# A LoRA block on one core: weights that arrive transposed, activations turned in transpose mode, a split shared with GpSimd

## The chip, the cores and the metric

One core of a Trainium2 chip runs the kernel. The metric is the device time of one execution in microseconds; the time before is the median of 3 runs. TensorE is PE in the profile, with PEld for its weight loads; VectorE is DVE, ScalarE is ACT, GpSimd is POOL, and SyncE, which issues most transfers, is SP.

## What is computed

Eight sequences of 128 tokens with 512 features (`x`) pass through four adapter layers. Each sequence picks its own adapter. All data is float32.

```python
w = L0_weight[id0]                          # (8, 512, 512), one matrix per sequence, stored (out, in)
x = x + einsum('bsi,boi->bso', x, w)        # layer 0; the result is x1 below
# layer 1: q, k, v = x1 @ W + (x1 @ A[id1]) @ B[id1];  q, k turned by rope(pos);  causal, masked softmax; out projection
x = x + attention(x, mask, pos, id1)
x = x + einsum('bnr,bor->bno', einsum('bni,bri->bnr', x, L2_B[id0]), L2_A[id0])     # layer 2, rank 16
x = x + x @ L3_W.T + L3_b + 2 * (x @ L3_As[id2]) @ L3_Bs[id2]                       # layer 3, rank 16
```

## The kernel before

Every large product is made of three fp32r products of TensorE, each of a high and a low half: `hi*hi + hi*lo + lo*hi`. The high half is a copy to fp32r by ScalarE, the low half is the difference, by VectorE or GpSimd. So every operand passes through a "split". TensorE contracts over partitions, so a matrix whose rows are the wrong way round is first "turned": four matmuls of a 128x128 tile against an identity into one PSUM bank, from which the split reads.

The program has four blocks, one after the other, each closed by a barrier over the engines. Every engine has its own instruction order, written out by hand, and engines wait for each other by semaphores.

**Stage one (layer 0 and the preparation of layer 1).** The loop runs over b, the eight sequences, in a software pipeline. On PE, step b is: turn x and the weight of sequence b+1 (`transposes`, line 277, into the ring `ps_ring` of three banks: five "tiles", x and the four column blocks of the weight), `product(b)` (lines 288 to 290, twelve matmuls of 512 columns), turn x1 of b-1 (line 298), `adapters(b-2)` (lines 309 to 311) and `turn_ax(b-3)` (line 321). ScalarE makes all five high halves of a sequence (line 347), VectorE all five low halves (line 401); they read the PSUM ring. Between these VectorE makes rope tables: `angles` reduces the angle in seven passes over 128x1024 for the sine, and once more in eight passes, with a quarter turn added, for the cosine. SP loads the weights (1 MB each) into two buffers `w0_raw`; the load for b waits until the weight of b-2 has been turned. It also loads x, three adapter pieces of 32 KB per sequence in rows of 64 bytes (`a_raw`), and after b = 4 the first block of layer 1's weights and adapters (`raw_w`, `raw_b`, 1 MB each). GpSimd only issues transfers here: 16 gathers of `bk` and `bv` rows, then 16 gathers of `bq` and `ao` (256 KB each) from DRAM to DRAM, as fast as it can.

**Stage two** projects k and v, **stage three** (lines 787 to 1135) is the attention loop over 8 heads by 8 sequences. Neither is touched by the change, but for a table read.

**The last stage** does layers 2 and 3. On PE: gather of the adapter rows (1264), turns of layer 3's weight and of `l2b_sel` (1238), a small product m of the adapters (1272), the product c (1280 to 1284) into one bank, eight products of the out adapter (1289), eight turns of x2 (1238), then `narrow` (1257 to 1303) and the eight wide products (1308 to 1315). VectorE has in order: the low halves of `w3t`, `bo_pack` (1384), the copy `cm` of c (1407), the eight sums into `res` (1363), the low halves of x2 (1412), `m_pack` (1415), `own` (1371). GpSimd makes `l3a_lo` (1436) and adds the bias (1441).

Of the kernel before, what the change touches and what calls it, by code (L numbers as in the profile page):

```python
# [31 lines left out]
def program(nc, x, lora_ids, pos, attn_ids, slot_ids, mask, w0, wq, wk, wv, wo, aq, bq, ak, bk, av, bv, ao, bo,  # L32
            l2a, l2b, w3, b3, l3a, l3b, ident_c, causal_c, rope_c, gather_c, twin_c, out):
# [13 lines left out]
    R = aq.shape[2]  # L47
# [20 lines left out]
    with whole:  # L68
# [34 lines left out]
        l2b_sel = sb(whole, "l2b_sel", [P, HID])  # L103
        l2a_sel = sb(whole, "l2a_sel", [P, KC, B, R])
        l3a_sel = sb(whole, "l3a_sel", [P, KC, B, R])
# [15 lines left out]
        rope_cols = sb(attn, "rope_cols", [P, 3])  # L121
# [34 lines left out]
        with ExitStack() as c:  # L156
# [14 lines left out]
            ps_ring = [ps(c, f"ps_ring{i}", [P, HID]) for i in range(3)]  # L171
            ps_y = [ps(c, f"ps_y{i}", [P, HID]) for i in range(2)]
            ps_x1 = ps(c, "ps_x1", [P, KC, T])
# [15 lines left out]
            tile_ready = sem(c, "tile_ready")  # L189
            tile_hi_done = sem(c, "tile_hi_done")  # L190
            tile_lo_done = sem(c, "tile_lo_done")
# [14 lines left out]
            TILES = 1 + KC  # L206

            with nc.Block() as block:
                @block.sync
                def _(sp):  # L210
# [3 lines left out]
                    for b in range(B):  # L214
                        a = sp.value_load(id_rows[0:1, 0, b:b + 1], min_val=0, max_val=w0.shape[0] - 1)
                        if b >= 2:

                            sp.wait_ge(tile_ready, TILES * (b - 1))
                        src = w0[bass.DynSlice(a, 1), :, :].rearrange("a (c p) i -> p (a c) i", p=P)
                        if b == 0:  # L220

                            for k in range(KC):
                                cols = slice(k * P, (k + 1) * P)
                                sp.dma_start(w0_raw[0][:, :, cols], src[:, :, cols]).then_inc(w0_first_in[k], 16)
# [5 lines left out]
                        pick = sp.value_load(id_rows[0:1, 1, b:b + 1], min_val=0, max_val=aq.shape[0] - 1)  # L230
                        for n, src in enumerate((aq, ak, av)):
                            sp.dma_start(a_raw[:, b, :, n, :],
                                         src[bass.DynSlice(pick, 1)].rearrange("a (c p) r -> p (a c) r", p=P)).then_inc(a_in[b], 16)
# [8 lines left out]
                def _(pool):  # L242
# [1240 lines left out]
```

## Time and profile before

| | before |
|---|---|
| median of 3 runs | 849.56 us (848.63 to 849.73) |
| span of the profiled execution | 850.1 us |
| TensorE busy | 797.7 us, 94% |
| VectorE, ScalarE, GpSimd busy | 621.6, 363.9, 307.9 us |
| stage one | 0 to 106 us |
| stages two and three | 106 to 782 us |
| last stage | 782 to 850 us |

The profiled execution has no time of its own beside its span; the span, 850.1 us, is 0.5 us above the median of the runs. A row of instruction groups reads: line, engine, operation, output <- input, shapes, count | busy us, mean ns of one | idle us just before them and what ended it. A float32 matmul stands as two records, an fp32r one as one. A row of busy time by stretch reads: the stretch, its length, busy us (instructions) of PE, PEld, DVE, ACT and POOL, the granted TensorE clock as a share of full speed, the busy share of the 16 DMA engines, GB/s. A row of a timeline: start us, us from the first to the last instruction merged in it, engine, line, operation, names, shapes, count, and in brackets the idle time before it and what ended it.

### The profile page before, as it was taken

The page shows a single profiled execution, that of the slowest core. Times are in us where ns is not written, and L with a number is a line of the kernel's source. Part 1 is how long each engine was busy: PE and PEld are TensorE (multiplying, and loading weights), DVE is VectorE, ACT ScalarE, POOL GpSimd, SP SyncE. Part 2 cuts the span into 40 slices and gives each one's busy share as a digit, 9 for nine tenths or more (in the row PEclk, how much of TensorE's full clock was granted, in tenths as well). Part 3 has the DMA queues.
Part 4 walks back from the last instruction along what each step waited for, and adds up shares of the span by engine and source line. Part 5 has one row for each costly group of instructions (what it writes and reads, how often), then busy time and mean ns, then how long its engine had stood idle before and what let it go on. Part 6 is the DMA issues. An engine that isn't in the chain of part 4 may idle for free. (4 is left out here: it accounts for less than half of the span.)

```text
span 850.1 us, 14916 instructions
## 1 busy us (share of the span) xinstructions
PE 797.7 (94%) x4780; PEld 674.6 (79%) x4780; DVE 621.6 (73%) x1556; ACT 363.9 (43%) x989; POOL 307.9 (36%) x261
## 2 busy tenths in 40 slices
PE   5699898999779999999999999999999999987898
PEld 5599786778568888888888888888888888865786
DVE  2568652488669789779779878878877977864783
ACT  3245442311054446446446446446445544543450
POOL 5300030044455336337336426435524632510220
PEclk9899999999989999999999999999999999999899
DMA  9992178887405123313304402602512211601302
GB/s 270 315 276 57 46 195 225 225 218 205 136 2 130 44 63 72 104 42 81 111 0 118 116 0 67 168 0 62 135 38 62 62 37 43 128 7 35 94 13 86
DMA packets 112750, 86.89 MB, mean 102 GB/s; under 512 B 60534, under 2 KB 79126, under 8 KB 112454
## 3 DMA queue, kind: packets, MB, share of 16 engines
q1 hardware_dynamic: 110770, 79.83, 35.7%
q0 software_dynamic: 1792, 6.49, 2.3%
q8 instruction: 21, 0.34, 0.2%
q14 instruction: 19, 0.16, 0.1%
q10 hardware_dynamic: 148, 0.07, 0.0%
HBM read 71.40 MB, written 20.73 MB: 108 GB/s over the span
## 5 line engine op out<-in xcount | busy, mean ns | idle before, releaser
L935 POOL TENSOR_TENSOR prob<-prob,rinv 128x512 f32<-128x512 f32 x64 | 66.7, 1042 | 198.6 <-DVE rinv L1025 198.6
L880 ACT ACTIVATE prob<-sm,nmax 128x128 f32<-128x128 f32 x256 | 99.8, 391 | 81.0 <-DVE nmax L1006 81.0
L928 POOL TENSOR_TENSOR qt<-qc,qs 128x512 f32<-128x512 f32 x60 | 96.0, 1599 | 94.8 <-DVE qs L964 94.8
L1102 PE MATMUL ps_out<-wo_hi,ot_hi 128*128 128x512 f32 x256 | 106.2, 415 | 5.4 <-DVE ot_lo L983 3.7
L1104 PE MATMUL ps_out<-wo_hi,ot_lo 128*128 128x512 f32 x256 | 100.6, 393 | 0.0
L82 PE MATMUL ps_q<-x1t_hi,blk_hi 128*128 128x512 f32 x240 | 100.5, 419 | 0.0
L1103 PE MATMUL ps_out<-wo_lo,ot_hi 128*128 128x512 f32 x256 | 99.6, 389 | 0.0
L1006 DVE CUSTOM_DVE_ANT_0 sm<-ps_s,maskbias 128x128 f32<-128x128 f32 x256 | 58.7, 284 | 53.8 <-issue 53.8
L83 PE MATMUL ps_q<-x1t_lo,blk_hi 128*128 128x512 f32 x240 | 95.5, 398 | 0.0
L84 PE MATMUL ps_q<-x1t_hi,blk_lo 128*128 128x512 f32 x240 | 95.2, 397 | 0.0
L964 DVE TENSOR_TENSOR qs<-ps_q,sin_t 64x512 f32<-64x512 f32 x120 | 82.6, 688 | 3.7
L869 ACT ACTIVATE ot_hi<-ps_o 128x512 fp32r<-128x512 f32 x64 | 38.1, 595 | 105.5 <-PE ps_o L1090 105.3
L1070 PEld LDWEIGHTS ps_s<-kt,qt 128*128 128x128 f32 x512 | 68.5, 195 | 11.0 <-issue 5.4
L1070 PE MATMUL ps_s<-kt,qt 128*128 128x128 f32 x512 | 69.2, 279 | 5.2 <-PEq L563 5.2
L1035 DVE TENSOR_TENSOR p_lo<-prob,p_hi 128x512 f16<-128x512 f32 x64 | 60.9, 951 | 5.9 <-ACT p_hi L896 4.1
L1102 PEld LDWEIGHTS ps_out<-wo_hi,ot_hi 128*128 128x128 f32 x256 | 48.1, 188 | 14.4 <-DVE ot_lo L983 4.9
L1104 PEld LDWEIGHTS ps_out<-wo_hi,ot_lo 128*128 128x128 f32 x256 | 48.0, 188 | 11.3
L863 ACT ACTIVATE pt_hi<-ps_t 128x512 fp32r<-128x512 f32 x64 | 38.3, 599 | 42.7 <-PE ps_t L1080 42.7
L1103 PEld LDWEIGHTS ps_out<-wo_lo,ot_hi 128*128 128x128 f32 x256 | 48.4, 189 | 8.5
L84 PEld LDWEIGHTS ps_q<-x1t_hi,blk_lo 128*128 128x128 f32 x240 | 45.4, 189 | 10.9
L896 ACT ACTIVATE p_hi<-prob 128x512 f16<-128x512 f32 x64 | 40.1, 627 | 29.0 <-POOL prob L935 28.8
L82 PEld LDWEIGHTS ps_q<-x1t_hi,blk_hi 128*128 128x128 f32 x240 | 45.7, 191 | 8.4
(207 smaller groups left out, 1937.1 us busy)
## 6 DMA issues: line engine op xcount, KB each, us to landing
wo_raw<-in_L_cond_wo SPq DMA_DIRECT2D x8, 1024.0 KB, 5.6
raw_w<-in_L_cond_wq SPq DMA_DIRECT2D x8, 1024.0 KB, 6.8
w_raw<-in_L_cond_weight SPq DMA_DIRECT2D x7, 1024.0 KB, 6.6
raw_b<-bq_sel SPq DMA_DIRECT2D x56, 128.0 KB, 4.6
raw_b<-bkv_sel SPq DMA_DIRECT2D x16, 256.0 KB, 6.7
v_hi_d<-v_hi SPq DMA_DIRECT2D x16, 256.0 KB, 3.7
v_lo_d<-v_lo SPq DMA_DIRECT2D x16, 256.0 KB, 4.9
k_rot<-kr SPq DMA_DIRECT2D x16, 256.0 KB, 2.6
```

Source lines behind the costliest of these rows:

```text
L82: pe.matmul(bank[:, :], w_hi[:, k, cols], x1t_hi[:, k, tok], start=(k == 0), stop=False)
L83: pe.matmul(bank[:, :], w_hi[:, k, cols], x1t_lo[:, k, tok], start=False, stop=False)
L84: pe.matmul(bank[:, :], w_lo[:, k, cols], x1t_hi[:, k, tok], start=False, stop=False)
L880: e = act.activation(prob[i][:, h, :], sm[:, h, :], ACT.Exp, bias=nmax[i][:, h:h + 1], scale=-1.0, accum_out=rsum[i][:, h:h + 1])
L928: pool.tensor_tensor(qt[:, half, h, :], qc[:, :], qs[:, :], ALU.add).then_inc(q_done, 1)
L935: pool.tensor_tensor(prob[i][:, :, :], prob[i][:, :, :], rinv[i][:, :].unsqueeze(2).broadcast_to([P, G, T]), ALU.mult).then_inc(prob_done, 1)
L964: dve.tensor_tensor(qs[to:to + 64, :], ps_q[i][at:at + 64, :], sin_t[to:to + 64, tok], ALU.mult).then_inc(q_mult, 1)
L1035: dve.tensor_tensor(p_lo[:, :, :], prob[i][:, :, :], p_hi[:, :, :], ALU.subtract).then_inc(p_lo_done, 1)
L1070: mm = pe.matmul(ps_s[b % 2][:, h, :], qt[:, half, h, at:at + T], kt[:, b * T:(b + 1) * T], start=True, stop=True)
L1102: pe.matmul(ps_out[:, :], ot_hi[:, q], wo_hi[:, h, :], start=(h == 0), stop=False)
L1103: pe.matmul(ps_out[:, :], ot_hi[:, q], wo_lo[:, h, :], start=False, stop=False)
L1104: pe.matmul(ps_out[:, :], ot_lo[:, q], wo_hi[:, h, :], start=False, stop=(h == G - 1))
```

## The change

- The host lays four tensors out as the core wants them: layer 0's weights (`w0t`), layer 3's weight (`w3t`) and layer 2's B transposed, and all adapter pieces in chunks, so that a partition's data is one run (8 KB for a weight; 768 bytes for the three adapter pieces, now one transfer). The turns of these weights on PE are gone, and their splits read SBUF, not PSUM.
- The turns of x, x1 and x2 stay, now as `pe.transpose` and not as a matmul with the identity. x and x1 have two PSUM banks each.
- Low halves of layer 0's weight: VectorE makes blocks 0 and 2, GpSimd blocks 1 and 3. The load of weight b waits for both low halves of b-2. GpSimd's gathers now stand between these, two sequences' worth behind each pair of low halves: `bk`, `bv` in steps 0 to 3, `bq`, `ao` in steps 4 to 7.
- The first block of layer 1 is loaded after b = 5 and not 4.
- The cosine is made from the sine's angle, sin(pi/2 - |angle|): one more pass on VectorE in place of eight.
- Last stage: no turns of `w3` and `l2b`; GpSimd makes `l2b_lo`.

```diff
                     for b in range(B):
-                            sp.wait_ge(tile_ready, TILES * (b - 1))
-                        src = w0[bass.DynSlice(a, 1), :, :].rearrange("a (c p) i -> p (a c) i", p=P)
+                            sp.wait_ge(wt_lo_done, 2 * (b - 1))
+                            sp.wait_ge(wt_lo_pool, 2 * (b - 1))
+                        src = w0t[bass.DynSlice(a, 1), :, :, :].rearrange("a p c o -> p (a c) o")
...
-                        if b == 4:
+                        if b == 5:
                             sp.wait_ge(gathered_kv, 2 * B * 16)
                             load_block_w(sp, 0)
                             load_block_b(sp, 0)
...
                     for b in range(B):
-                        a = pool.value_load(id_rows[0:1, 1, b:b + 1], min_val=0, max_val=bq.shape[0] - 1)
-                        pick = bass.DynSlice(a, 1)
-                        pool.dma_start(bkv_sel[b:b + 1, :, 0, :], bk[pick]).then_inc(gathered_kv, 16)
-                        pool.dma_start(bkv_sel[b:b + 1, :, 1, :], bv[pick]).then_inc(gathered_kv, 16)
...
+                        for k in (1, 3):
+                            pool.wait_ge(wt_hi_done, KC * b + k + 1)
+                            pool.tensor_tensor(wt_lo[b % 2][:, k, :], w0_raw[b % 2][:, k, :], wt_hi[b % 2][:, k, :].bitcast(F32),
+                                               ALU.subtract).then_inc(wt_lo_pool, 1)
+                        for n in (2 * b, 2 * b + 1):
+                            if n < B:
+                                gather_kv(n)
+                            else:
+                                gather_qo(n - B)
...
-                                mm = pe.matmul(ps_ring[m % 3][:, n * P:(n + 1) * P], src, ident[:, :], start=True, stop=True)
...
+                            mm = pe.transpose(ps_x[b % 2][:, k * T:(k + 1) * T], res[:, b, k * P:(k + 1) * P], ident[:, :])
...
                         for k in range(KC):
-                            pe.wait_ge(tile_lo_done, TILES * b + k + 2)
+                            if k % 2 == 0:
+                                pe.wait_ge(wt_lo_done, 2 * b + k // 2 + 1)
+                            else:
+                                pe.wait_ge(wt_lo_pool, 2 * b + k // 2 + 1)
...
                     pe.wait_ge(w3_in, 48)
...
-                    for k in range(KC):
-                        turn(k, [raw_w[:, o, k * P:(k + 1) * P] for o in range(KC)])
                     pe.wait_ge(l2_in, 32 * B)
-                    turn(L2B, [l2b_sel[:, k * P:(k + 1) * P] for k in range(KC)])
```

PE's order at the start of stage one, in the kernel before (`w_raw` is `w0_raw`; the second x and its weight are turned ahead of the first product):

```order
L277 MATMUL ps_ring<-ident,res 128x128 x4
L277 MATMUL ps_ring<-ident,w_raw 128x128 x16
L277 MATMUL ps_ring<-ident,res 128x128 x4
L277 MATMUL ps_ring<-ident,w_raw 128x128 x16
L288 MATMUL ps_y<-wt_hi,xt_hi 128x512
L289 MATMUL ps_y<-wt_lo,xt_hi 128x512
L290 MATMUL ps_y<-wt_hi,xt_lo 128x512
```

The same place in the changed kernel, with the waits:

```order
L281 MATMUL ps_x<-ident,res 128x128 [waits x_in1]
L281 MATMUL ps_x<-ident,res 128x128 x3
L295 MATMUL ps_y<-wt_hi,xt_hi 128x512 [waits wt_lo_done,xt_lo_done]
L296 MATMUL ps_y<-wt_lo,xt_hi 128x512
L297 MATMUL ps_y<-wt_hi,xt_lo 128x512
L295 MATMUL ps_y<-wt_hi,xt_hi 128x512 [waits wt_lo_pool]
L296 MATMUL ps_y<-wt_lo,xt_hi 128x512
```

Sixteen matmuls of weight turns per sequence are gone from PE, and every second group of three in a product waits for GpSimd. GpSimd's own order in the changed kernel, one step with a `bk`, `bv` pair of gathers (`TENSOR_LOAD` reads the adapter's number, `DMA` issues a gather):

```order
L262 TENSOR_TENSOR wt_lo<-w_raw,wt_hi 128x512 [waits wt_hi_done] x2
L243 TENSOR_LOAD id_rows
L243 ISA x2
L245 ISA
L245 DMA bkv_sel<-in_L_cond_bk 16x1024
L246 DMA bkv_sel<-in_L_cond_bv 16x1024
L243 TENSOR_LOAD id_rows
L243 ISA x2
L245 ISA
L245 DMA bkv_sel<-in_L_cond_bk 16x1024
L246 DMA bkv_sel<-in_L_cond_bv 16x1024
L262 TENSOR_TENSOR wt_lo<-w_raw,wt_hi 128x512 [waits wt_hi_done] x2
```

Before, this stretch held the gathers alone. Now two subtractions stand ahead of each two sequences' gathers, and the next subtractions behind them. PE in the last stage, in the changed kernel; before, 20 turns stood ahead of these rows:

```order
L1287 MATMUL ps_h<-w3t_hi,l2a_hi 128x512 [waits w3t_lo_done]
L1288 MATMUL ps_h<-w3t_lo,l2a_hi 128x512
L1289 MATMUL ps_h<-w3t_hi,l2a_lo 128x512
L1291 MATMUL ps_h<-ident,l2a_sel 128x128 x4
L1296 MATMUL ps_wide<-bo_pack,axo_pack 128x512 [waits bo_lo_done] x3
L1296 MATMUL ps_wide<-bo_pack,axo_pack 128x512 [waits wide_done,bo_lo_done] x5
```

The product c now follows the splits, which wait only for the data in SBUF.

## Rows read from the trace of the kernel before

**Rows 1.** Busy time by stretch: stage one and the last stage

```profile
0.00:106.00 106.00, 85.50 (x600) 79.92 (x600) 62.96 (x119) 42.09 (x90) 18.86 (x40) 0.95 0.66 192
782.00:850.00 68.00, 61.73 (x356) 52.13 (x356) 42.97 (x74) 22.88 (x46) 11.27 (x9) 0.95 0.25 71
```

**Rows 2.** Groups by form, PE, stage one: the weight turns

```profile
L277 PE MATMUL ps_ring<-ident,w_raw 128*128 128x128 f32 x256 | 34.1, 296 | 13.5 <-DMA w_raw<-in_L_cond_weight 12.9 <-DVE xt_lo L401 0.5
```

**Rows 3.** Timeline of PE, the first weight and one step: start, duration, instructions

```profile
9.17 5.87 PE L277 MATMUL ps_ring<-ident,w_raw 128*128 128x128 f32 x32 [3.12 <-DMA w_raw<-in_L_cond_weight]
...
62.79 3.74 PE L277 MATMUL ps_ring<-ident,w_raw 128*128 128x128 f32 x32
66.28 0.48 PE L288 MATMUL ps_y<-wt_hi,xt_hi 128*128 128x512 f32 x1
...
69.14 1.05 PE L298 MATMUL ps_x<-ident,res 128*128 128x128 f32 x8
69.94 0.27 PE L309 MATMUL ps_a<-a_hi,x1t_hi 128*128 128x48 f32 x1
...
71.28 0.53 PE L321 MATMUL ps_at<-ident_r,axn 128*128 128x128 f32 x3
```

**Rows 4.** Busy time by stretch: transfers while the weights arrive

```profile
0.00:60.00 60.00, 42.61 (x283) 39.73 (x284) 30.32 (x48) 20.43 (x34) 18.86 (x40) 0.94 0.98 286
60.00:72.00 12.00, 12.00 (x97) 11.48 (x96) 9.92 (x20) 5.45 (x13) 0.00 (x0) 1.00 0.69 192
20.00:40.00 20.00, 13.47 (x96) 12.27 (x94) 13.20 (x19) 6.18 (x11) 7.53 (x14) 0.93 0.95 334
```

**Rows 5.** Transfers of the weights, from issue to landing

```profile
DMA to landing us min/median/max: 6.1/6.6/16.9
```

**Rows 6.** Timeline of POOL: two gathers one sequence apart

```profile
5.32 0.51 POOL L251 DMA_DIRECT2D bkv_sel<-in_L_cond_bk  x1 [1.52 <-issue]
...
6.96 0.49 POOL L251 DMA_DIRECT2D bkv_sel<-in_L_cond_bk  x1 [0.64 <-issue]
```

**Rows 7.** POOL's subtractions of 512 columns in stage three: min/median/max ns of one

```profile
L920 POOL TENSOR_TENSOR blk_lo<-raw_w,blk_hi x28: 1284/1734/1764, 245.4 to 674.9; 128x512 fp32r<-128x512 f32 x28
```

**Rows 8.** Timeline of PE: end of stage one; first matmuls of stage two

```profile
94.47 1.05 PE L298 MATMUL ps_x<-ident,res 128*128 128x128 f32 x8
...
106.61 0.63 PE L705 MATMUL ps_p<-blk_lo,x1t_hi 128*128 128x512 f32 x1
107.04 0.63 PE L706 MATMUL ps_p<-blk_hi,x1t_lo 128*128 128x512 f32 x1
```

**Rows 9.** Timeline of PE, last stage

```profile
784.20 5.46 PE L1238 MATMUL ps_turn<-ident,raw_w 128*128 128x128 f32 x32
...
800.84 7.92 PE L1238 MATMUL ps_turn<-ident,res 128*128 128x128 f32 x64
808.51 0.36 PE L1257 MATMUL ps_h<-x2t_hi,l2b_hi 128*32 128x256 f32 x1
```

**Rows 10.** Timeline of DVE, last stage

```profile
784.08 1.61 DVE L1392 SCALAR_TENSOR_TENSOR axo_pack<-axo_pack,twin,ps_h 128x512 fp32r<-128x512 f32 x2 [0.42 <-ACT axo_pack L1334]
...
796.33 0.69 DVE L1407 COPY cm<-ps_h 128x512 f32<-128x512 f32 x1
...
810.15 1.29 DVE L1415 TENSOR_TENSOR m_pack<-m_raw,m_pack 64x128 fp32r<-64x128 f32 x1
```

**Rows 11.** Timeline of ACT, last stage: copies of 512 columns back to back

```profile
791.09 2.19 ACT L1340 ACTIVATE bo_pack<-raw_b 128x512 fp32r<-128x512 f32 x4
```

**Rows 12.** Timeline of PE: fp16 passes of 128 columns, back to back

```profile
756.92 0.22 PE L1080 MATMUL ps_t<-ident_h,p_lo 128*128 128x128 f16 x1
756.98 0.22 PE L1079 MATMUL ps_t<-ident_h,p_hi 128*128 128x128 f16 x1
```

**Rows 13.** Busy time by stretch: PE's granted clock in the last stage

```profile
784.00:786.00 2.00, 2.00 (x12) 1.80 (x12) 1.50 (x2) 0.92 (x3) 0.00 (x0) 0.72 1.02 250
786.00:788.00 2.00, 2.00 (x11) 2.00 (x11) 0.69 (x1) 0.89 (x2) 0.00 (x0) 0.50 1.06 230
```

More of the change, by code:

```diff
@@ L29, with program @@
 LORA_SCALE = 2.0
-def program(nc, x, lora_ids, pos, attn_ids, slot_ids, mask, w0, wq, wk, wv, wo, aq, bq, ak, bk, av, bv, ao, bo,
-            l2a, l2b, w3, b3, l3a, l3b, ident_c, causal_c, rope_c, gather_c, twin_c, out):
+def program(nc, x, lora_ids, pos, attn_ids, slot_ids, mask, w0t, wq, wk, wv, wo, a_qkv, bq, bk, bv, ao, bo,
+            l2a_l, l2b_l, w3t, b3, l3a_l, l3b, ident_c, causal_c, rope_c, gather_c, twin_c, out):
     B, T, HID = x.shape
@@ L46, in program @@
     G = wq.shape[1] // wk.shape[1]
-    R = aq.shape[2]
+    R = bq.shape[1]
     NT = B * T
@@ L170, in program @@
             axn = [sb(c, f"axn{i}", [P, 3, 4, 2, R], F32R) for i in range(2)]
-            ps_ring = [ps(c, f"ps_ring{i}", [P, HID]) for i in range(3)]
+            ps_x = [ps(c, f"ps_x{i}", [P, KC * T]) for i in range(2)]
             ps_y = [ps(c, f"ps_y{i}", [P, HID]) for i in range(2)]
-            ps_x1 = ps(c, "ps_x1", [P, KC, T])
+            ps_x1 = [ps(c, f"ps_x1{i}", [P, KC, T]) for i in range(2)]
             ps_a = ps(c, "ps_a", [P, 3, R])
@@ L262, in _, with turn_x @@
                 def _(pe):
-                    def transposes(b):
+                    def turn_x(b):
                         pe.wait_ge(x_in[b], 16)
@@ L294, in turn_x1 @@
                         pe.wait_ge(x1_done, b + 1)
-                        if b >= 1:
-                            pe.wait_ge(x1t_lo_done, b)
+                        if b >= 2:
+                            pe.wait_ge(x1t_lo_done, b - 1)
                         for k in range(KC):
-                            mm = pe.matmul(ps_x1[:, k, :], res[:, b, k * P:(k + 1) * P], ident[:, :], start=True, stop=True)
+                            mm = pe.transpose(ps_x1[b % 2][:, k, :], res[:, b, k * P:(k + 1) * P], ident[:, :])
                         mm.then_inc(x1t_ready, 1)
@@ L1233, in _, with turn @@
                 def _(pe):
-                    def turn(n, tiles):
-                        if n >= 3:
-                            pe.wait_ge(turn_lo_done, n - 2)
-                        for k, tile in enumerate(tiles):
-                            mm = pe.matmul(ps_turn[n % 3][:, k * P:(k + 1) * P], tile, ident[:, :], start=True, stop=True)
+                    def turn(b):
+                        if b >= 3:
+                            pe.wait_ge(turn_lo_done, b - 2)
+                        for k in range(KC):
+                            mm = pe.transpose(ps_turn[b % 3][:, k * P:(k + 1) * P], res[:, b, k * P:(k + 1) * P], ident[:, :])
                         mm.then_inc(turn_ready, 1)
@@ L1291, in _ @@
                         pe.wait_ge(wide_done, b + 1)
-                        turn(X2 + b, [res[:, b, k * P:(k + 1) * P] for k in range(KC)])
+                        turn(b)
                     pe.wait_ge(m_done, PAIRS)
+                    pe.wait_ge(l2b_lo_done, 1)
                     pe.wait_ge(c_done, 1)
@@ L1454, in constants @@
     root = float(HEAD_DIM) ** -0.25
-    rope = np.zeros((P, 3), np.float32)
+    rope = np.zeros((P, 4), np.float32)
+    rope[:, 3] = np.pi / 2
     rope[:, 0] = np.concatenate([freq, freq])
@@ L1472 @@
     arrays, args = {}, []
-    for name, a in [(n, inputs[n]) for n in _INS] + list(constants().items()):
+    given = {n: np.asarray(a) for n, a in inputs.items()}
+    for name, a in layouts(given) + list(constants().items()):
         a = np.ascontiguousarray(a)
```

238 lines of the change are left out of this document (127 added, 111 removed).

## Prediction

> **What bounds the kernel now.** I read the busy time by stretch first, to see which part the change can reach. Stage one lasts 106 us with PE 85.5 us busy, the last stage 68 us with PE 61.7 us busy [rows 1]; the 676 us between them hold no changed work. Then the groups of PE in stage one: the weight turns alone are 256 records and 34.1 us, and the idle time before them, 13.5 us, was ended 12.9 us by the weight's transfer [rows 2]. Then PE's timeline, to see what one step costs back to back: weight turn 62.79 to 66.28, 3.49 us; product to 69.14, 2.86 us; turn of x1 to 69.94, 0.80 us; adapters to 71.28, 1.34 us; adapter turn some 0.4 us [rows 3]; the turn of x, the same form as that of x1, 0.8 to 0.95 us. The sum is 9.8 us a step. From 60 to 72 us PE is busy all the time and sets the pace; before, the transfers do: to 60 us the DMA engines are 98% busy at 286 GB/s [rows 4]. So stage one has two bounds, PE and, right under it, the transfers. The last 11.6 us, from the end of the last product at 94.47 [rows 8] to the start of stage two at 106 [rows 1], are a chain of short dependent pieces.
>
> **Stage one, PE.** Removed: 3.49 us a step. The turns that stay lose something: four float32 turns take 0.80 us now [rows 3], 0.2 us each in two passes. The trace has no transpose mode. Bounds: no gain (0.80), or the pace of fp16 passes of the same 128 columns, one each 0.06 us [rows 12], so 0.24 for four. I take 0.45, between them. A step is then 2.86 + 1.34 + 0.4 + 2 x 0.45 = 5.5 us (5.1 to 6.2). If PE alone counted, eight steps would save 8 x 4.3 = 34 us, plus most of the 12.9 us of waits.
>
> **Stage one, GpSimd.** It now does in every step two subtractions and two sequences' gathers, in order, and the product waits for both subtractions. One sequence's gathers take 6.96 - 5.32 = 1.64 us [rows 6], so 3.3 us a step. A subtraction of 512 columns takes 1.28 to 1.76 us in stage three [rows 7], the high end where VectorE is at work beside it. VectorE is 59% busy in stage one and loses seven table passes and half of the weight splits, so I take 1.4 us, nearer the low end. The step is 3.3 + 2.8 = 6.1 us (5.9 to 6.8), longer than PE's 5.5. GpSimd becomes the pacer.
>
> **Stage one, transfers.** What moves up to the last weight was 286 GB/s x 60 us + 192 x 12 = 19.5 MB [rows 4]. Now 2.1 MB of it, the last four `bq`, `ao` pairs, are issued behind the last weights' splits: 17.4 MB stay ahead. At 286 GB/s that is 61 us, at the best 20 us stretch, 334 GB/s [rows 4], 52 us. The adapter pieces come in 768-byte runs, not 64-byte ones, and the burst of 4.2 MB of gathers, through which one weight took 16.9 us to land where the median is 6.6 [rows 5], is spread out. I take 57 us. The 2 MB of `raw_w`, `raw_b` stand ahead of the last two weights, so the wait is at sequence 6; I count it in the 57.
>
> **Stage one, the walk.** The first weight piece is there at 9.17 [rows 3]; the others follow, and ScalarE splits each on arrival, in 0.55 us [rows 11]. GpSimd ends step 0 at about 13. The second weight, issued about 10.5 (one adapter transfer ahead of it instead of three), lands at 17; steps 1 to 5 end at 21, 27, 33, 39, 45. Weight 6 lands one step's 1.36 MB (4.5 us) before weight 7, at 52.5, and needs 0.55 x 2 + 2 x 1.4 = 3.9 us of splits: step 6 ends at 56.4, step 7 at 56.4 + 6.1 = 62.5 (its weight, there at 57, is not late). The last three matmuls end at 63.2. VectorE and ScalarE have some 4.5 us of work a step (more while tables are made) and hide in 6.1. The tail is of the same pieces, 11.6 us: it keeps its length. Stage two starts at 74.8 instead of 106: **31 us saved**. Seven fewer table passes give nothing: they lie on VectorE, which isn't the pacer; without the cover of GpSimd's 6.1 us they would count 0.7 to 1.4 us each, since a copy of half their width takes 0.69 [rows 10].
>
> **Last stage.** The turns of `w3` and `l2b` go: from 784.20 to about 790.4 on PE [rows 9]. But c needs the splits, and ScalarE and VectorE reach them only behind `axo_pack`, done at 785.7 [rows 10]. Four low halves then take 2.5 us. PE, idle from 784.2, starts m at 785.8 and c at about 786.6; its clock was granted 0.72 and 0.50 in these four microseconds even with the turns running [rows 13], so I count c's 2.8 + 0.9 us at half speed in part: c ends at 792 (790.5 to 794.5) instead of some 795. `cm` on VectorE moves from 796.33 to about 792.6 behind `bo_pack`: 3.7 us earlier (1.5 to 4.5). The eight turns of x2, 800.84 to 808.51, 0.96 us each on PE [rows 9], fall under the pace of ScalarE, 12 copies at 0.55 [rows 11] or 6.6 us: another 1.1 to 1.7 us. `m_pack`, which opens the chain that `narrow` waits for, comes at about 805 instead of 810.15 [rows 10], and from there PE is full to the end. **5 us saved** (3 to 6).
>
> **Sum.** 850.1 - 31.2 - 5 = 813.9 us of span; less the 0.5 us by which the profiled span stands above the median of the runs, 813.4. I say 814.
>
> **The clock.** What stays on PE in the idle parts are transposes. The clock in this trace is granted in full from 60 to 72 us, where PE is busy all the time [rows 4], and is at its lower level, 1.2 GHz, when PE has had little to do, as in the first matmuls of stage two, 0.43 us for 512 columns [rows 8]. The Trainium skill, page "TensorE: Matmul & The Clock Gate", Part 4, says that transpose mode does not count as PE busy for the clock. No row here can show it. By that rule the eight turns of x2 would leave `narrow` at the half clock; rival 2 is the same thing at its full size. The same page, Terms, calls transpose mode four times faster for float32; an estimate by that figure, 0.80 / 4 = 0.20 us for four, puts PE's step at 5.0 us and leaves the sum as it is, since GpSimd paces.
>
> **Rivals.**
> 1. *The transfers pace.* If the 17.4 MB move at 270 GB/s, the last weight lands at 64.5; splits 3.9, matmuls 0.7, tail 11.6: stage two at 81, saving 25 + 5: **820 us**. For it: 98% busy before. Against: fewer small packets, no burst.
> 2. *PE stays at its half clock in stage one,* because it now idles between groups. Steps at half speed: product 12 x 0.43 = 5.2 us, adapters 2.3, turns 1.5, adapter turn 0.7, so 9.7 us. Stage one is 13 + 8 x 9.7 + 14 (tail, partly slow) = 105 at worst, some 98 if the clock comes back now and then, which I take; with 2 us from the last stage **840 us**. Against: PE would be 5.5 of 6.1 us busy.
> 3. *GpSimd doesn't pace,* its subtractions at 1.28 us and transfers at 334 GB/s: the last weight at 52, PE's 5.5 us a step. Stage two at 52 + 3.7 + 0.7 + 11.6 = 68, saving 38 + 6: **806 us**.
> 4. *Slower:* the subtractions on GpSimd and VectorE's on the same SBUF data hold each other up. Each of 16 subtractions is on the path; to lose the 36 us each must take 1.4 + 36 / 16 = 3.65 us. The longest of 28 is 1.76 [rows 7]. Above 3.65 us the kernel is slower, at 4 us **855 us**.
>
> **How the numbers follow.** Chances: forecast 0.58 (its own range 808 to 819), rival 1 0.17, rival 2 0.08, rival 3 0.14, rival 4 0.02, nothing gained 0.01. Leaving out rival 2, rival 4 and the outer half of rival 3 gives 803 to 826. What a measurement of this kernel can tell from no change is 0.2%, 1.7 us: faster 0.97, same 0.01, slower 0.02.
>
> **What would show it.** Stage two's first matmul at 75 (70 to 82). No `w_raw` turns on PE; four turns in 0.24 to 0.80 us. GpSimd's subtractions near 1.4 us, and PE's idle time before the products ended by GpSimd's `wt_lo` in steps 1 to 5, by a weight's transfer (through ScalarE) at 6. Last stage: c's copy near 792.6 less the shift of stage one, span from it to the end 5 us less. Wrong: if PE's idle time is ended by transfers throughout, or its clock stands at 0.5 over stage one, or if stages two and three change length by more than 2 us, for which I have no reason.

## The result, and the profile after

The changed kernel takes 829.5 us (median of 4 runs, 825.83 to 831.85) against 849.6 us for the kernel before: a ratio of 0.976, 95% interval 0.9732 to 0.9789. It is faster, but by 20 us and not by the forecast 36. Its profiled execution has a span of 830.2 us at a mean granted clock of 0.965. One profiled execution of all that follow, e7's, was disturbed (1445 us, where its other four took 808 to 811); it is left out of the ratio, and its trace is not read.

The balance by stage, from the first matmul of each stage in the two traces:

| | stage one | stages two and three | last stage | span |
|---|---|---|---|---|
| before | 106.05 | 676.3 | 67.8 | 850.1 |
| after | 89.06 | 678.5 | 62.7 | 830.2 |
| gain | 17.0 | -2.2 | 5.1 | 19.9 |

The last stage gave what was forecast. Stage one was to end at 74.8 and ends at 89.06: 14.3 of the 16 us that are missing lie there.

Busy time by stretch of the changed kernel, to be read beside [rows 4] (stretch, its length, busy time of PE, PEld, DVE, ACT, POOL with instruction counts, granted clock, DMA share, GB/s):

```profile
0.00:60.00 60.00, 35.54 (x182) 29.47 (x182) 40.11 (x55) 28.18 (x55) 33.37 (x45) 0.91 0.85 285
20.00:40.00 20.00, 13.03 (x74) 10.39 (x72) 19.79 (x22) 8.68 (x20) 14.28 (x18) 0.91 0.73 249
24.00:32.00 8.00, 6.24 (x28) 4.78 (x29) 7.97 (x8) 1.98 (x4) 5.91 (x10) 0.79 0.53 136
```

Two things to see. VectorE is busy for 19.79 of 20 us in the middle of stage one, with 22 instructions; before it was 13.2 us with 19. And the transfers, at 334 GB/s there before, run at 249, with a hole of 136 GB/s from 24 to 32 us. So neither GpSimd, nor TensorE, nor the transfers had this stretch full: VectorE had. In the next 20 us it is the transfers that are full, with a share of 1.00 at 324 GB/s:

```profile
40.00:60.00 20.00, 12.88 (x71) 11.26 (x71) 11.56 (x23) 9.44 (x19) 7.26 (x10) 0.82 1.00 324
```

What PE waited for ahead of the first matmul of each group of three in a product (us in total, times), over all eight sequences:

```profile
its engine sat idle before it (us, times) until:
  DVE wt_lo L418: 12.6, 6
  DVE xt_lo L412: 12.0, 4
  POOL wt_lo L262: 0.2, 1
```

The forecast wanted GpSimd's `wt_lo` here. It ended 0.2 us of idle time; VectorE's low halves ended 24.6.

Timeline of GpSimd in the changed kernel, then of VectorE (start, duration, instruction, count; in brackets the idle time before it and what ended it):

```profile
20.91 2.48 POOL L262 TENSOR_TENSOR wt_lo<-w_raw,wt_hi 128x512 fp32r<-128x512 f32 x2
25.51 2.51 POOL L262 TENSOR_TENSOR wt_lo<-w_raw,wt_hi 128x512 fp32r<-128x512 f32 x2
...
59.61 2.97 POOL L262 TENSOR_TENSOR wt_lo<-w_raw,wt_hi 128x512 fp32r<-128x512 f32 x2 [10.03 <-ACT wt_hi L361]
...
64.68 2.50 POOL L262 TENSOR_TENSOR wt_lo<-w_raw,wt_hi 128x512 fp32r<-128x512 f32 x2
```

```profile
19.15 0.69 DVE L460 TENSOR_SCALAR turns<-ang 128x1024 f32<-128x1024 f32 x1
19.88 4.08 DVE L461 TENSOR_SCALAR turns<-turns 128x1024 f32<-128x1024 f32 x1
23.99 0.69 DVE L412 TENSOR_TENSOR xt_lo<-ps_x,xt_hi 128x512 fp32r<-128x512 f32 x1
24.60 3.98 DVE L418 TENSOR_TENSOR wt_lo<-w_raw,wt_hi 128x512 fp32r<-128x512 f32 x2
...
64.12 4.15 DVE L475 TENSOR_TENSOR maskbias<-maskbias,causal 128x1024 f32<-128x1024 f32 x1
68.31 0.69 DVE L412 TENSOR_TENSOR xt_lo<-ps_x,xt_hi 128x512 fp32r<-128x512 f32 x1
```

Read the two side by side by their ends. L460 and L461 are the same kind of pass over the same 1024 columns; one takes 0.69 us, the other 4.08, and it ends at 23.96, 0.57 us behind GpSimd's pair (20.91 + 2.48 = 23.39). The two `wt_lo` that should take 1.28 us take 3.98 and end at 28.58, behind the pair that ends at 28.02. The mask pass ends at 68.27, behind the pair that ends at 67.18. `xt_lo`, one operand of which lies in PSUM, takes 0.69 us each time. VectorE is "busy" in these rows, and is standing. One thing does not fit: L461 starts 1.03 us before the pair, while GpSimd issues gathers, and could have been over; why it was not is open.

What comes of it in this trace, in SP's queue and on ScalarE: weight 4 is issued only at 28.79, when VectorE's low halves of weight 2 are done, and weight 6 at 41.86. ScalarE's splits of weight 6 start at 58.38, 16.5 us after the issue:

```profile
28.79 0.34 SPq L228 DMA_DIRECT2D w_raw<-in_L_cond_weight_t  x1
...
41.86 0.36 SPq L228 DMA_DIRECT2D w_raw<-in_L_cond_weight_t  x1
```

```profile
42.79 2.18 ACT L361 ACTIVATE wt_hi<-w_raw 128x512 fp32r<-128x512 f32 x4
58.38 2.19 ACT L361 ACTIVATE wt_hi<-w_raw 128x512 fp32r<-128x512 f32 x4 [7.90 <-DMA w_raw<-in_L_cond_weight_t]
```

PE at the end of stage one, beside [rows 8]:

```profile
69.74 0.69 PE L295 MATMUL ps_y<-wt_hi,xt_hi 128*128 128x512 f32 x1 [3.39 <-DVE wt_lo L418]
70.23 0.63 PE L296 MATMUL ps_y<-wt_lo,xt_hi 128*128 128x512 f32 x1
70.66 0.63 PE L297 MATMUL ps_y<-wt_hi,xt_lo 128*128 128x512 f32 x1
...
73.93 0.40 PE L297 MATMUL ps_y<-wt_hi,xt_lo 128*128 128x512 f32 x1
...
79.77 0.87 PE L305 MATMUL ps_x<-ident,res 128*128 128x128 f32 x4
...
83.00 0.38 PE L316 MATMUL ps_a<-a_hi,x1t_hi 128*128 128x48 f32 x1 [1.83 <-DVE axn L446]
...
89.06 0.76 PE L710 MATMUL ps_p<-blk_hi,x1t_hi 128*128 128x512 f32 x1 [0.96 <-PEq L210]
```

The last product waits 3.39 us for VectorE's `wt_lo`, which stood behind the mask pass. It starts at the lower clock (0.43 us a matmul) and ends at 74.2. From there to stage two it is 14.9 us, where it was 11.6. The last turn of x1 (79.77) comes late, and the last adapters wait for what follows it.

Last stage, PE and VectorE, beside [rows 9, 10]: from the stage's first matmul at 767.54, `cm` comes after 10.8 us (before: 14.0) and `narrow` after 20.8 (before: 26.2).

```profile
767.54 1.95 PE L1275 MATMUL ps_h<-axo,row_gather 32*128 32x512 f32 x4 [1.24 <-PEq L793]
...
788.29 0.35 PE L1268 MATMUL ps_h<-x2t_hi,l2b_hi 128*32 128x256 f32 x1
```

```profile
778.34 0.69 DVE L1413 COPY cm<-ps_h 128x512 f32<-128x512 f32 x1 [0.39 <-PE ps_h L1291]
```

### The profile page after: what moved, and what is told of

Read it like the earlier page. It is cut to its first block and busy times, and to the rows that moved or that the text cites. A ratio compares the mean times of both kernels' runs of the same rounds, so it can differ in the third digit from the quotient of the medians.

```text
span 830.2 us, 14084 instructions
## 1 busy us (share of the span) xinstructions
PE 761.6 (92%) x4388; PEld 633.7 (76%) x4388; DVE 613.0 (74%) x1532; ACT 361.3 (44%) x989; POOL 333.5 (40%) x278
## 5 line engine op out<-in xcount | busy, mean ns | idle before, releaser
L1041 DVE TENSOR_TENSOR p_lo<-prob,p_hi 128x512 f16<-128x512 f32 x64 | 57.6, 900 | 5.9 <-ACT p_hi L902 4.1
L985 DVE TENSOR_TENSOR pt_lo<-ps_t,pt_hi 128x512 fp32r<-128x512 f32 x64 | 44.2, 690 | 10.9 <-ACT pt_hi L869 8.9
```

## The experiments

Fourteen runs, each with one trace. All but m1 edit the changed kernel; "the four edits" are e1, e2, e3 and e5 in one kernel (runs e7 and e8). Medians are compared by the ratio to the kernel before on the same chip, and 1% is 8.5 us. "Product" is the start of the last matmul of the eighth product, "tail" the time from there to stage two's first matmul, all in us.

| run | median | ratio (95% interval) | product | stage two from | tail | stages two, three |
|---|---|---|---|---|---|---|
| kernel before | 849.6 | 1 | 94.24 | 106.05 | 11.8 | 676.3 |
| changed kernel | 829.5 | 0.9760 (0.9732 to 0.9789) | 73.93 | 89.06 | 15.1 | 678.5 |
| e1 all low halves on VectorE | 827.0 | 0.9723 (0.9680 to 0.9765) | 69.31 | 86.83 | 17.5 | 675.4 |
| e2 block 1 loaded last | 820.1 | 0.9622 (0.9566 to 0.9677) | 61.72 | 78.31 | 16.6 | 678.4 |
| e3 mask table in step 9 | 825.9 | 0.9712 (0.9663 to 0.9761) | 68.51 | 84.10 | 15.6 | 677.6 |
| e5 turn of x1 first | 821.8 | 0.9645 (0.9615 to 0.9675) | 69.28 | 81.90 | 12.6 | 681.4 |
| e6 no transpose mode | 826.8 | 0.9709 (0.9678 to 0.9739) | 69.68 | 87.70 | 18.0 | 677.6 |
| e4 first three together | 813.1 | 0.9571 (0.9519 to 0.9622) | 57.45 | 74.05 | 16.6 | 674.2 |
| e7 all four | 809.8 | 0.9507 (0.9480 to 0.9534) | | | | |
| e8 the same | 810.7 | 0.9511 (0.9455 to 0.9566) | 55.03 | 69.94 | 14.9 | 675.6 |
| e9 four, share and mask back | 815.4 | 0.9582 (0.9531 to 0.9634) | 61.62 | 74.24 | 12.6 | 674.7 |
| e13 four, block 1 early again | 821.3 | 0.9657 (0.9625 to 0.9689) | 68.04 | 80.65 | 12.6 | 673.5 |
| e10 four, fillers | 810.1 | 0.9500 (0.9446 to 0.9553) | 55.64 | 70.00 | 14.4 | 676.4 |
| e11 four, angles late | 812.4 | 0.9525 (0.9478 to 0.9571) | 54.84 | 70.58 | 15.7 | 678.5 |
| e12 e10, gathers awaited later | 808.3 | 0.9499 (0.9475 to 0.9522) | 55.33 | 68.21 | 12.9 | 672.5 |

The last column holds no edit but in e12 (a wait moved there), and spreads from 673.5 to 681.4 without it. So the 2.2 us that stages two and three seemed to lose are not to be told from none.

**e1: GpSimd's share taken back.**

```diff
-                        for k in (1, 3):
-                            pool.wait_ge(wt_hi_done, KC * b + k + 1)
-                            pool.tensor_tensor(wt_lo[b % 2][:, k, :], ...)
+                        pool.wait_ge(wt_lo_done, KC * (b + 1))
...
-                        for k in (0, 2):
+                        for k in range(KC):
                             dve.wait_ge(wt_hi_done, KC * b + k + 1)
```

> The changed kernel with all four low halves of w0's splits on VectorE; GpSimd only issues its gathers, two sequences a step, behind VectorE's last low half of the step. Theory A (VectorE's passes over SBUF stand still while GpSimd's subtractions read SBUF; 14 us of VectorE's 59 busy us in stage one are such standing): no VectorE instruction of 128x512 or 128x1024 above 1.3 us, VectorE busy about 59 - 14 + 16 x 0.62 = 55 us, w0(4) issued at 25 or earlier instead of 28.8, stage two's first matmul at 82 to 86 instead of 89.06, span 823 to 827. Rival B (the transfers pace stage one, the standing is hidden): first matmul within 1.5 us of 89. Rival C (VectorE's own work becomes the pacer, some 6.5 us a step): PE's idle time before the products ended by VectorE in most steps, first matmul at 88 to 92.

The group of `wt_lo` in e1 (min/median/max ns of one) and ScalarE's step 6, then for comparison VectorE's group in the changed kernel:

```profile
L411 DVE TENSOR_TENSOR wt_lo<-w_raw,wt_hi x32: 681/684/693, 9.2 to 67.5; 128x512 fp32r<-128x512 f32 x32
```

```profile
57.95 2.19 ACT L354 ACTIVATE wt_hi<-w_raw 128x512 fp32r<-128x512 f32 x4 [13.75 <-DMA w_raw<-in_L_cond_weight_t]
```

```profile
L418 DVE TENSOR_TENSOR wt_lo<-w_raw,wt_hi x16: 680/692/3387, 9.4 to 69.5; 128x512 fp32r<-128x512 f32 x16
```

The standing is gone: the longest of 32 is 0.693 us, where one of 16 took 3.387. The place was right and the gain small: weight 6, behind block 1's loads, still lands at 57.95, and ScalarE now waits 13.75 us for it. Stage two starts 2.2 us earlier, and the intervals of the two medians overlap. A cure that ends in another wait shows little by itself; e9 prices it below. Nor did VectorE become free: from 20 to 40 us it is busy for 19.79 us as before, now with 37 instructions, and the transfers there run at 246 GB/s. So its work fills this stretch without any standing, and the lower rate of the transfers is not shown to come from the standing.

**e2: block 1's loads behind weight 7.**

```diff
-                        if b == 5:
+                        if b == 7:
                             sp.wait_ge(gathered_kv, 2 * B * 16)
                             load_block_w(sp, 0)
                             load_block_b(sp, 0)
```

> The changed kernel with the loads of block 1 of the projections (raw_w, raw_b, 2 MB) issued behind w0(7) instead of ahead of w0(6). Theory B (w0(6) took 16.5 us from issue to landing because 2 MB stood ahead of it): it lands 4 to 6 us earlier, ScalarE's wait of 7.90 us ahead of step 6 falls to 2 to 4 us, stage two's first matmul at 84 to 86 instead of 89.06. Rival (the pace comes from VectorE and PE after step 6 anyway, or ScalarE now waits for raw_w in step 7 or the tail): first matmul at 87.5 to 90.

ScalarE's splits of weights 6 and 7:

```profile
47.05 2.19 ACT L361 ACTIVATE wt_hi<-w_raw 128x512 fp32r<-128x512 f32 x4 [0.60 <-DMA w_raw<-in_L_cond_weight_t]
53.62 2.19 ACT L361 ACTIVATE wt_hi<-w_raw 128x512 fp32r<-128x512 f32 x4 [1.55 <-DMA w_raw<-in_L_cond_weight_t]
```

Weight 6 is split 11.3 us earlier, at 47.05, more than expected, and stage two starts at 78.31, 10.75 us earlier. An estimate of what the 2 MB take at the 324 GB/s of the changed kernel is 6.5 us, so the edit does more than take them out of the way. One more part is on record: the loads of block 1 wait for the `bk` and `bv` gathers (4.9 us of SP's time in e13, which has this order too), and weight 6 stands behind that wait; in e13 it is issued at 40.59, in e8 at 37.13. How the rest divides was not run. By its median this is the largest of the single edits, though its interval overlaps that of e5.

**e3: the mask table out of step 5,** moved from `b == 5` to `b == 9`.

> The changed kernel with the two passes of the mask table on VectorE moved from step 5 to step 9, behind the last pack_ax. Theory A: the pass that took 4.15 us at 64.1, while GpSimd subtracts, no longer stands ahead of xt_lo(7) and wt_lo(7); product(7) starts 3 to 4 us earlier (69.7 in the changed kernel) and ends at 70 to 71.5; stage two's first matmul at 85 to 87, the mask pass itself 1.2 us. Rival: product(7) is bound by PE's half clock and by GpSimd's wt_lo(7), done at 67.2: first matmul within 1 us of 89.

Stage two starts 5 us earlier, but the reading must be weaker: in e5 and e6, where the mask pass stands in step 5 as in the changed kernel, it took 1.22 us and not 4.15, and the product came 4.2 to 4.7 us earlier too. So the gain here is not shown to be the edit's. Which passes stand changes from one trace to the next; with one trace a kernel it can't be said how much of that is the edit and how much the execution. The medians, 829.5 and 825.9, are the better measure and their intervals overlap.

**e4: e1, e2 and e3 together.**

> The three edits together. Theory A plus B, if the gains add: 4 + 4 + 2 us, stage two's first matmul at 78 to 81, span about 820. If one pace lies under the others (VectorE's work of some 6.5 us a step, or PE at half clock in its idle parts): first matmul at 82 to 86.

Stage two starts at 74.05, better than expected, and the kernel is at 813.1: stage two starts 15.0 us earlier, where the three by themselves gave 17.9, so the gains add for the most part. The tail is still 16.6 us.

**e5: turn of x1 ahead of the adapters.** The list of the change leaves one thing out: the change had put `adapters(b - 2)` ahead of `turn_x1(b - 1)`:

```diff
-                        if 2 <= b <= B + 1:
-                            adapters(b - 2)
                         if 1 <= b <= B:
                             turn_x1(b - 1)
+                        if 2 <= b <= B + 1:
+                            adapters(b - 2)
```

> The changed kernel with turn_x1(b - 1) ahead of adapters(b - 2) on PE again, as it stood before the change. Theory D (in the tail adapters(5), then adapters(6), stand ahead of turn_x1(6) and turn_x1(7), whose splits the next adapters wait for; that is why the tail from the end of product(7) to stage two's first matmul is 14.9 us where it was 11.6): it falls to 12 to 13 us, stage two's first matmul at 86 to 87.5 if product(7) ends at 74.2 as now. Rival (the tail is longer by PE's half clock alone, 0.43 instead of 0.23 us a matmul): the tail stays at 14.5 us or more. What happens ahead of the tail: nothing for either.

PE at the end of stage one:

```profile
69.51 0.60 PE L305 MATMUL ps_x<-ident,res 128*128 128x128 f32 x4
...
71.57 0.62 PE L305 MATMUL ps_x<-ident,res 128*128 128x128 f32 x4
...
81.90 0.77 PE L710 MATMUL ps_p<-blk_hi,x1t_hi 128*128 128x512 f32 x1 [0.97 <-PEq L210]
```

The last two turns of x1 now follow the last product by 0 and 2 us; in the changed kernel they came at 75.42 and 79.77, 1.3 and 5.6 us behind its end. The tail is 12.6 us, and it is 12.6 in every kernel with this order that does not wait for something else (e9, e13). With the adapters first it is 15.1 in the changed kernel, the shortest of its kind: 15.6 to 18.0 in e1, e2, e3, e4 and e6. Stage two starts 7.2 us earlier, more than expected, and the median, with an interval apart from that of the changed kernel, is 9.8 us better by the ratios. The cleanest pair is e2 and e9, which differ in this order alone: the product at 61.72 and 61.62, stage two at 78.31 and 74.24, so 4.1 us, all of it in the tail, and 3.4 us by the ratios, whose intervals overlap. Why e5 gains more than that is not settled.

**e6: what the transpose mode is worth.** `pe.transpose` put back to a matmul with the identity in the three places.

> The changed kernel with the turns of x and x1 in stage one and of x2 in the last stage as matmuls with the identity instead of transpose mode. Price of the mode: four turns 0.80 us instead of 0.45. If the mode only shortens work that PE waits beside anyway: stage one within 1.5 us of the changed kernel's 89.06, last stage longer by 0 to 3 us. If transposes keep PE's clock down (a turn by matmul would keep it up): the granted clock over 20 to 100 us rises from 0.81 to over 0.9, and the kernel becomes faster by 2 us or more.

The medians do not differ beyond their intervals. Stage one is 1.4 us shorter in its trace and the last stage 2.5 us longer (830.5 - 765.29 = 65.2), as the first reading said; the granted clock over 20 to 100 us is 0.83 against 0.81, far from the 0.9 of the rival, so the mode is not what keeps the clock down.

**m1: the disputed costs by themselves.**

> Nothing of the reference is computed: x is copied to the output, and the disputed costs are run by themselves. VectorE runs six passes of a kind (128x512 subtraction of two SBUF tiles; the same with one operand in PSUM; tensor_scalar over 128x1024 in SBUF; scalar_tensor_tensor over 128x1024) while GpSimd runs three subtractions of 128x512 or four DRAM gathers. Theory A: with both operands in SBUF, and with tensor_scalar, passes stand for whole subtractions of GpSimd (a group of six takes its own time plus some 3.9 us, the three subtractions); with one operand in PSUM nothing is lost (0.69 us each). Rival: both slow down a little (VectorE 0.69 to 1.0 us, GpSimd 1.27 to 1.7 us) and neither stands. TensorE: four transposes in 0.45 us; if transposes keep the clock down, the first matmuls of 512 columns behind 200 transposes come 0.43 us apart, and 0.23 us apart behind 100 turns by matmul.

VectorE's six passes of each kind: two SBUF operands alone, the same beside GpSimd, one operand in PSUM, tensor_scalar beside GpSimd, tensor_scalar beside gathers. Then GpSimd's three subtractions: alone, beside the passes with two SBUF operands, and beside those with one in PSUM:

```profile
12.66 3.70 DVE L101 TENSOR_TENSOR do<-xs,hi 128x512 f32<-128x512 f32 x6 [2.31 <-POOL so L120]
...
20.82 6.92 DVE L101 TENSOR_TENSOR do<-xs,hi 128x512 f32<-128x512 f32 x6 [0.20 <-POOL so L120]
...
28.14 3.68 DVE L103 TENSOR_TENSOR do<-ps_s,hi 128x512 f32<-128x512 f32 x6 [0.20 <-POOL so L120]
...
32.22 6.95 DVE L105 TENSOR_SCALAR do<-res 128x1024 f32<-128x1024 f32 x6 [0.20 <-POOL so L120]
...
50.11 3.76 DVE L105 TENSOR_SCALAR do<-res 128x1024 f32<-128x1024 f32 x6 [0.20 <-POOL so L120]
```

```profile
16.76 3.73 POOL L131 TENSOR_TENSOR pool_out<-xs,hi 128x512 fp32r<-128x512 f32 x3
...
20.75 4.64 POOL L131 TENSOR_TENSOR pool_out<-xs,hi 128x512 fp32r<-128x512 f32 x3
...
28.06 3.76 POOL L131 TENSOR_TENSOR pool_out<-xs,hi 128x512 fp32r<-128x512 f32 x3
```

Apart, the six and the three need 3.70 + 3.73 = 7.43 us; started together they need 6.99 (20.75 to 27.74). That is the sum of the two but for 0.4 us, as if they ran one after the other. With one operand in PSUM neither notices the other (3.68 and 3.76 us). Gathers hold nothing up (3.76). One more kind, scalar_tensor_tensor over 1024 columns, took 10.14 us beside the subtractions, which took 5.73; it was not run alone. The Trainium skill, page "SBUF — State Buffer", section "Who interferes with whom", states this as an exclusive lock: a VectorE pass with two SBUF inputs contends with a GpSimd instruction that reads SBUF, as does one in a 2-port mode, which tensor_scalar can enter, and the one that comes second waits for the whole instruction. This run agrees with it for each kind of pass that stood or didn't stand beside the subtractions.

TensorE in m1: 200 transposes of 128x128 (one record each), forty products behind them, and after a pause 100 turns by matmul (two records each); below, the granted clock over the transposes, over the first products, and in the pause, when TensorE has had nothing since 44.3:

```profile
L145 PE MATMUL ps_t<-ident,xs x200: 272/273/421, 12.2 to 35.0; 128*128 128x128 f32 x100
L151 PE MATMUL ps_t<-ident,xs x200: 275/275/582, 73.0 to 98.2; 128*128 128x128 f32 x100
```

```profile
16.00:32.00 16.00, 16.00 (x149) 16.00 (x147) 11.27 (x18) 0.00 (x0) 12.36 (x12) 1.00 0.00 1
36.00:44.00 8.00, 8.00 (x37) 6.56 (x35) 7.66 (x7) 0.00 (x0) 5.38 (x5) 1.00 0.00 0
48.00:50.00 2.00, 0.00 (x0) 0.00 (x0) 1.77 (x3) 0.00 (x0) 0.03 (x1) 0.61 0.00 0
52.00:72.00 20.00, 0.00 (x0) 0.00 (x0) 18.30 (x26) 0.00 (x0) 12.76 (x17) 0.50 0.04 12
```

A transpose takes 22.8 us / 200 = 0.114 us, four 0.46; a turn by matmul 25.2 us / 100 = 0.25, the first of them at the lower clock (four were 0.80 in [rows 3]). Through 23 us of nothing but transposes the granted clock stayed at 1.00, and the products behind them, forty in 9.33 us, came 0.23 us apart at 2.4 GHz. With nothing to do since 44.3 it began to fall between 48 and 50 us and stood at 0.50 for the rest of the pause. So transposes held a full clock up; the reading alone would not show it, since it is 1.00 in the first 10 us of this trace too, before TensorE has any work. Whether they raise one that has fallen was not run.

**e7 and e8: all four edits.** e8 is the kernel of e7 once more, for its trace.

> All four low halves on VectorE, block 1's loads behind w0(7), the mask table in step 9, and turn_x1 ahead of adapters. Theory D: the tail, 16.5 us in the kernel with the first three edits, falls by 2.5 to 4 us, stage two's first matmul from 74.05 to 70 to 71.5, span 808. Rival: no more than 1 us off 74.05.

> The kernel of the four edits once more, for its trace (the profiled execution of the first was a disturbed one): stage two's first matmul at 70 to 71.5, span 806 to 810.

809.8 and 810.7 us. In e8 stage two starts at 69.94, as expected, though the tail is 14.9 us and not 12.6:

```profile
69.94 0.77 PE L703 MATMUL ps_p<-blk_hi,x1t_hi 128*128 128x512 f32 x1 [3.26 <-PEq L210]
```

PE has nothing from 66.7 to 69.9. Stage one ends with a wait for the `bq` and `ao` gathers, and its last transfers end at 68.3. PE has become so early that this wait shows. VectorE is now the full engine: 38.6 of the 40 us from 20 to 60, with nothing standing.

**e9: two undone, the share and the mask table as in the changed kernel.**

> The changed kernel with block 1's loads behind w0(7) and turn_x1 ahead of adapters, but the low halves still shared with GpSimd and the mask table in step 5. Theory A (GpSimd's subtractions cost VectorE more than they take off it): 3 to 7 us longer than the kernel of the four edits, 812 to 816, stage two's first matmul at 73 to 77, VectorE busy for all of 20 to 60 us. Rival (with the transfers out of the way the share is as good): within 1.5 us of 809.

0.9582 against 0.9507, 6.4 us slower, as theory A said, with intervals that just touch; the four times of e9, 813.5 to 819.6, all lie above the two of e8. Half of the weight splits on GpSimd cost more than they give; what part of it is the mask table's was not run apart. VectorE's own `wt_lo` show it best, summed over their rows: 32 of them take 19.9 us in e8, and in the changed kernel the 16 that are left take 16.7, while GpSimd spends 23.7 us on the others.

**e13: one undone, block 1's loads ahead of weight 6 again.**

> The kernel of the four edits with one of them undone: block 1's loads stand ahead of w0(6) again. If the load order is the largest term and the others can't pay while it stands: stage two's first matmul at 80 to 83, 9 us or more above the 809 of the four edits. Rival (with VectorE free of GpSimd and the weights issued earlier the 2 MB fit in between): within 3 us of 809.

ScalarE's step 6 in e13:

```profile
57.01 2.19 ACT L354 ACTIVATE wt_hi<-w_raw 128x512 fp32r<-128x512 f32 x4 [13.50 <-DMA w_raw<-in_L_cond_weight_t]
```

0.9657 against 0.9507, 12.8 us: the largest term, from this side. Undoing the turn order is e4, 0.9571, 5.4 us. The three sum to 24.6 us, for a distance from the changed kernel of 21.5 (0.9760 - 0.9507): within the intervals they add.

**e10 and e12: the clock of the tail.** e10 has 15 filling matmuls on PE:

```diff
+                        warm({B: 2, B + 1: 6, B + 2: 3}.get(b, 0))
                         if 2 <= b <= B + 1:
                             adapters(b - 2)
```

> The kernel of the four edits with 15 filling matmuls of 512 columns on TensorE in the idle parts of the tail (2, 6, 3 and 4 of them, into a bank that nothing reads any more). Theory E (the half clock costs the tail 1.3 us in adapters(7), 0.7 us in the adapter turns, and stage two 2.5 us in its first twelve matmuls): granted clock over the tail 0.9 or more, first matmuls of stage two 0.23 us apart, 3 to 4.5 us faster, 804 to 806. Rival (the clock falls all the same, or the fillers hold the adapters up): within 1.5 us of 809.

> The kernel of the four edits with the fillers of e10, and with the wait for the bq and ao gathers taken from the end of stage one to stage two, ahead of the first load that reads them. In the two kernels before, TensorE had nothing from 66.7 to 69.9 while the last of these transfers landed at 68.3, so the fillers could change nothing. Theory E with that wait gone: stage two's first matmul at 66 to 68, its first twelve matmuls at 0.23 us instead of 0.43, together 4 to 6 us, 804 to 806. Rival (stage two then starts into transfers that are still under way, and gives the time back there, as raw_b for its first block): the first matmul at 66 to 68, but the time within 1.5 us of 809.

In e10 the clock is held at 1.00 up to 68 us, where in e8 it was 0.59 and 0.50 from 60 on, and nothing is gained (810.1): PE waits for the gathers until 70.00 and falls back to the lower clock. With that wait moved into stage two (e12) it starts at 68.21, its matmuls 0.24 us apart:

```profile
68.21 0.47 PE L710 MATMUL ps_p<-blk_hi,x1t_hi 128*128 128x512 f32 x1 [1.81 <-PEq L210]
68.52 0.40 PE L711 MATMUL ps_p<-blk_lo,x1t_hi 128*128 128x512 f32 x1
```

The median is 808.3, ratio 0.9499 against 0.9507 and 0.9511: not to be told from the four edits, where theory E wanted 804 to 806. From 80 to 100 us PE is busy 16.4 us in e12 and 17.8 in e8, so part of the lead may be waited off again; that isn't settled.

**e11: the angle passes in steps 4 to 7.**

> The kernel of the four edits with the eight passes for the angles moved from steps 0 to 3 to steps 4 to 7, and the two sines from 3 and 4 to 7 and 8. If VectorE's full occupation from 14 to 47 us sets the pace there (it is busy 19.8 of 20 us from 20 to 40): w0(4) issued 4 us or more earlier, stage two's first matmul 2 to 4 us earlier. Rival (the passes cost the same wherever they lie, since VectorE paces to the end, or the transfers pace once VectorE doesn't): within 1.5 us of 809.

The rival was right: 812.4, ratio 0.9525, no gain. The transfers ran at 337 GB/s from 20 to 60 us instead of 303, and the last product came at 54.84 instead of 55.03. VectorE is busy for 17.5 of the 20 us from 20 to 40 and for 19.6 of the next 20: the passes fill it later instead of earlier.

The fastest kernel is that of the four edits, 810 us, with or without e12's additions: 19 to 22 us faster than the changed kernel (21.5 by the ratios).

## Why the prediction was wrong

The direction and the last stage were right, the size in stage one was not. 829.5 us lies between rival 1 (820) and rival 2 (840), and is neither.

- **Last stage, 5 us saved.** Measured 5.1. `cm` came 3.2 us earlier (forecast 3.7), `narrow` 5.4, so the part behind `cm` gave 2.2 (forecast 1.1 to 1.7). The mechanism was right; that the sum is met to 0.1 us is luck, two misses of half a microsecond that cancel.
- **The transposes, four in 0.45 us.** Measured 0.46 in m1. Right. In e6's trace they were worth 2.5 us in the last stage and nothing that shows in stage one.
- **Stages two and three unchanged.** They moved by 2.2 us, over the 2 us that were to show the forecast wrong. That sign was set too tight: the same code spreads from 673.5 to 681.4.
- **GpSimd at 6.1 us a step is the pacer.** Wrong. Two sequences' gathers took 2.0 to 2.5 us, not 3.3 (20.91 - 18.51, and 25.51 - 23.39 = 2.1), and a pair of subtractions 2.5 to 3.7. Where it had its inputs GpSimd ended steps 1 to 3 at 18.6, 23.4 and 28.0, earlier than the forecast 21, 27 and 33; then it waited, 5.69, 2.71 and 10.03 us, and it ended only 0.2 us of PE's idle time.
- **"VectorE and ScalarE have some 4.5 us of work a step (more while tables are made) and hide in 6.1".** Wrong twice. It sized VectorE's work too low: in e8, where nothing stands, a step is 7.0 us while tables are made (x's low halves at 19.84, 26.83 and 33.87), of which 1.24 are the two blocks that GpSimd has in the changed kernel; that leaves 5.8. And it left out the standing. Rival 4, with a chance of 0.02, had the mechanism and priced it as a longer subtraction on GpSimd, with the 1.76 us of [rows 7] as its limit. The bill came to VectorE instead: up to 3.4 us more for one of its passes, and late low halves. VectorE's low halves ended PE's waits of 4.74, 1.29 and 1.83 us ahead of the products at 25.4, 33.9 and 41.2.
- **The transfers, "I take 57 us", weight 6 "at 52.5".** The amount was right: 17.4 MB forecast, 285 GB/s x 60 us = 17.1 MB moved by 60 us. The rate of 305 GB/s behind the 57 was not: 285 is what the kernel before had in its first 60 us (286), with a slack stretch of 249 from 20 to 40 us, where VectorE was full, and a full one from 40 to 60. Weight 6, behind the 2 MB of block 1, was forecast at 52.5 and split from 58.4. In e13, which has neither the standing nor the new turn order, it is still split only from 57.0, so 4.5 us are this term's own; with the 2 MB behind it, it is split from 43.1 (e8). Rival 1 had the cause, and its 64.5 for weight 7 was above what came (splits begun at 62.2).
- **"The tail is of the same pieces, 11.6 us: it keeps its length".** The same pieces, in another order: the diff moves the turn of x1 behind the adapters, and I did not walk the tail with it. From the end of the last product it is 14.9 us where it was 11.6; by the table's measure 15.1, 12.6 with the order restored, and 11.8 before.
- **Rival 2, the half clock,** was partly there: 0.81 from 20 to 100 us, where it was 0.96 before. Its price was tried only in the mended kernel, where holding the clock up through the tail gave nothing measurable (e10, e12).

The steps that failed in the forecast's walk can be read at weight 6, where ScalarE's splits of it begin (the forecast's own number is its landing), in the traces that have block 1's loads ahead of it:

| | weight 6 from | from there to stage two |
|---|---|---|
| forecast | 52.5 | 22.3 |
| changed kernel | 58.4 | 30.7 |
| e6, the same order of work | 56.8 | 30.9 |
| e1, no share | 58.0 | 28.9 |
| e3, mask table late | 55.5 | 28.6 |
| e5, turn order restored | 57.0 | 24.9 |
| e13, all three | 57.0 | 23.6 |

The 14.3 us are then 4.5 for weight 6 landing late with the standing and the turn order mended, 1.4 more for it in the changed kernel (within the spread of this column), 5.8 for the turn order (30.7 to 24.9), 1.3 for the share and the mask table (24.9 to 23.6), and 1.3 that e13 keeps above the forecast. That weight 6 comes late and that the tail did not keep its length are most of it; the standing, which looks worst in the profile, is the least while block 1's loads stand in front. These are single traces: the first column alone spreads from 55.5 to 58.4. With the load order mended too, e8 starts at 69.94, under the forecast. That is no support for the walk: the pacer of e8 is VectorE, busy for 38.6 of the 40 us from 20 to 60, and not GpSimd.

## What to carry to other kernels

Before an elementwise pass goes from VectorE to GpSimd, look at what VectorE does at that time: if its passes read two SBUF tiles or are tensor_scalar over SBUF, the two engines take turns, and a pass of 0.62 us is traded for one of 1.24. Count what VectorE has left to do as well: here it was full from 20 to 40 us with the share and without it. In a profile this shows as a busy VectorE with few instructions, one of them several times its usual length, that ends with GpSimd's. Walk the drain of a pipeline with the new order of instructions, not only its steady step, and ask of each load what stands in the queue ahead of the one that is awaited.

## What was not expected of the hardware

- Six VectorE passes and three GpSimd subtractions over SBUF took 6.99 us together and 7.43 apart; which of them stand differs from one trace to the next (the mask pass: 4.15 us in the changed kernel, 1.22 in e5 and e6, which have the same instructions on both engines).
- The transpose mode did not lower TensorE's clock: 1.00 over 23 us of transposes alone. The Trainium skill, page "TensorE: Matmul & The Clock Gate", Part 4, says that the clock's full level does not engage for it and that it doesn't count as busy the same way; for float32 m1 does not agree as far as holding the clock goes. The mode is a little under twice as fast as a matmul turn, 0.114 us against 0.20 in [rows 3], not four times, as the same page of the Trainium skill has it under Terms.
